# The last feed-forward layer moves into the attention track, as products with tokens on partitions

## What is computed

```python
# layer 3, attention: ctx is 77 x 128, one head over all 128 features
x1 = relu(layernorm(x) @ W.T) * diagonal;  x2 = relu(ctx @ W.T)
x  = x + tanh(g_xattn[3]) * softmax(x1 @ x2.T + mask) @ ctx
# layer 3, feed-forward: 8 experts of 128 x 128, the two largest router weights are kept
y  = layernorm(x);  r = softmax(y @ W_router.T + b_router);  w = r where r is among its two largest, else 0
x  = x + tanh(g_ffn[3]) * sum_e w[:, e] * (y @ W_experts[e].T + b_experts[e])
```

## Time and profile before

| | us |
|---|---|
| median of 3 runs (lowest, highest) | 1231.35 (1228.35, 1235.36) |
| the profiled execution: its time | 1217.92 |
| the profiled execution: its span | 1216.2 |
| PE busy | 1002.3 (82%) |
| DVE busy | 688.4 (57%) |
| ACT busy | 461.2 (38%) |
| chain that ended last: PE, DVE, ACT | 56%, 24%, 9% |

### The profile page before, as it was taken

One profiled execution on the slowest core, in us unless ns is written; L12 is line 12 of the kernel. 1 busy time (PEld: TensorE's weight loads), 2 busy tenths in 40 slices (PEclk: granted clock), 3 DMA queues, 4 the chain that ended last, 5 costly groups with the idle time before them and its releaser, 6 DMA issues.

```text
span 1216.2 us, 14249 instructions
## 1 busy us (share of the span) xinstructions
PE 1002.3 (82%) x4727; PEld 642.2 (53%) x4727; DVE 688.4 (57%) x2092; ACT 461.2 (38%) x1097; POOL 105.6 (9%) x174
## 2 busy tenths in 40 slices
PE   2458889887877786875889989989989999999998
PEld 1334444443333465555556656757757677775442
DVE  0761442518266386378364565775775676766542
ACT  0514345357647454445522424425314322221110
POOL 2100000003022021022000000100100010000000
PEclk8569899999687798888898989999999999998765
DMA  9200000000000000000000000000000000000000
GB/s 273 81 1 1 1 1 1 1 1 1 0 1 0 1 1 1 1 1 1 1 1 1 1 1 1 1 1 1 1 1 1 1 1 1 1 1 1 9 9 18
DMA packets 12081, 12.73 MB, mean 10 GB/s; under 512 B 3766, under 2 KB 7912, under 8 KB 12008
## 3 DMA queue, kind: packets, MB, share of 16 engines
q10 hardware_dynamic: 5536, 8.04, 2.3%
q1 hardware_dynamic: 6088, 3.24, 1.0%
q0 software_dynamic: 384, 0.53, 0.2%
HBM read 10.75 MB, written 1.05 MB: 10 GB/s over the span
## 4 chain that ended last, share of the span: by engine, by line
PE 56%; DVE 24%; ACT 9%; issue 3%; POOL 1%; ACTq 0%; DVEq 0%
PE bank L1540 8%; PE bank L1528 5%; PE bank L1447 5%; PE bank L1530 4%; PE bank L1529 4%; DVE hb L1240 4%; PE bank L1582 4%; DVE nm L1105 3%; PE bank L1333 3%; PE bank L1467 3%; DVE hb L1244 3%; DVE x L1229 2%; ACT PTs L904 2%; ACT hb L938 2%; PE bank L1345 2%
## 5 line engine op out<-in xcount | busy, mean ns | idle before, releaser
L1240 DVE SCALAR_TENSOR_TENSOR hb<-hb,bank 96x512 f32<-96x512 f32 (+1 forms) x160 | 109.3, 683 | 177.1 <-ACT hb L938 176.6
L938 ACT ACTIVATE hb<-bank 96x512 f32<-96x512 f32 (+1 forms) x160 | 95.2, 595 | 291.2 <-PE bank L1530 291.0
L1540 PEld LDWEIGHTS bank<-m_w,hb 128*128 128x128 f32 (+1 forms) x1280 | 173.5, 199 | 24.5 <-DVE x L1229 6.0
L1540 PE MATMUL bank<-m_w,hb 128*128 128x128 f32 (+1 forms) x1280 | 176.6, 283 | 1.0
L1528 PE MATMUL bank<-parts,m_w_lo 128*96 128x512 f32 (+1 forms) x320 | 150.3, 470 | 13.0 <-DVE hb L1240 13.0
L1529 PE MATMUL bank<-parts,m_w_hi 128*96 128x512 f32 (+1 forms) x320 | 133.2, 416 | 0.0
L1530 PE MATMUL bank<-parts,m_w_hi 128*96 128x512 f32 (+1 forms) x320 | 132.9, 415 | 0.0
L1345 PE MATMUL bank<-KT,Qs 96*128 96x308 f32 x192 | 78.1, 425 | 42.5 <-ACT PTs L851 21.2
L1244 DVE TENSOR_TENSOR hb<-hb,bank 96x512 f32<-96x512 f32 (+1 forms) x160 | 109.7, 686 | 5.5
L1467 PE MATMUL bank<-Qs,KT 112*77 112x512 f32 x192 | 95.3, 527 | 16.5 <-ACT PTs L904 14.3
L1105 DVE TENSOR_REDUCE nm<-bank 128x4 f32<-128x308 f32 x192 | 83.6, 470 | 14.7 <-PE bank L1349 7.8
(11 more groups left out here) (269 smaller groups left out, 1530.2 us busy)
## 6 DMA issues: line engine op xcount, KB each, us to landing
nat_m<-in_L_ffn_W_dram ACTq DMA_DIRECT2D x1, 1408.0 KB, 16.8
m_w<-in_L_ffn_w_dram ACTq DMA_DIRECT2D x1, 1024.0 KB, 10.8
raw_w<-in_L_ffn_w_dram ACTq DMA_DIRECT2D x1, 1024.0 KB, 11.9
x<-in_x_dram SPq DMA_DIRECT2D x4, 256.0 KB, 9.0
out_dram<-x SPq DMA_DIRECT2D x4, 256.0 KB, 2.0
f_out<-in_L_ffn_Wout_dram POOLq DMA_DIRECT2D x8, 64.0 KB, 7.5
m_w<-in_L_ffn_W_experts_dram ACTq DMA_DIRECT2D x1, 512.0 KB, 16.6
ctxn<-in_ctx_dram SPq DMA_DIRECT2D x4, 38.5 KB
```

The lines of the kernel that those rows point to most:

```text
L938: act.activation(hb[n % 3][0:m, :], bank[TURN[0]][0:m, :], ACT.Tanh, scale=0.5).then_inc(*chunk_act.up(u, n))
L1240: dve.scalar_tensor_tensor(out=h, in0=h, scalar=1.0, in1=bank[TURN[0]][0:m, :], op0=ALU.add, op1=ALU.mult) \
L1540: op = pe.matmul(bank[7][:, t * P:(t + 1) * P], hb[n % 3][0:m, t * P:(t + 1) * P], wd, start=i == 0 and t == 0, stop=ends_expert(k, n) and ...
```

## The change

Layer 3 leaves the feed-forward track. The attention track now has the twelve attention halves of layers 0 to 2 and then, for each stream in turn, its layer-3 attention half and its layer-3 feed-forward half: A12 is layer-3 attention of stream 0, A13 layer-3 feed-forward of stream 0, A14 and A15 are those of stream 1, A16 and A17 of stream 2, A18 and A19 of stream 3. Beside F10 now lie four halves of that track (A12 to A15), beside F11 two (A16, A17), and A18 and A19 follow alone.

A layer-3 feed-forward half now has tokens on partitions. For each of the four tiles of 128 tokens and each group of four experts (`E3`), PE makes one 128 x 512 product in three fp32r passes into bank 0 or 1. DVE adds its four 128-column parts to `x`, each with its own token weight, in four instructions that wait for one another. The bias is one addition ahead of them. The gate is now folded into the token weights.

The weights `m3_w` get a high and a low part. To make room, `raw_w3` now lies in the memory of `m1_w2`, and the load of `m1_w2` is issued by ACT later, when POOL has read `raw_w3` for the last time.

```diff
+ATTENTIONS = 3 * STREAMS
 def kind(u):
     half, i = u
+    if half == "A" and i >= ATTENTIONS:
+        return "F3" if (i - ATTENTIONS) % 2 else "A3"
     return half + str(i // STREAMS)
...
-            raw_w3 = tmp("raw_w3", [P, MOE1, F1])[:]
+            raw_w3 = m1_w2[:].rearrange("p e c d -> p e (c d)")
...
-            grouped("m3", [(nat_e[:, e, :], m3_w[:, e, :]) for e in range(MOE3)])
+            split += split_parts("m3", nat_e, m3_w, MOE3)
...
                 act.dma_start(nat_m3[:], a["L2_ffn_W3"].rearrange("e m n -> m e n")).then_inc(*landed["m2_w3"].up("all", by=16))
-                act.dma_start(m1_w2[:], a["L1_ffn_w2"].rearrange("e (c p) d -> p e c d", p=P)) \
-                    .then_inc(*landed["rest"].up("all", by=16))
                 act.dma_start(graw[:, 0, :], a["g_xattn"].partition_broadcast(P)).then_inc(*landed["gates"].up(by=16))
...
                     if i == m2_last:
+                        act.wait_ge(*m1_low.at("m1_w3"))
+                        act.dma_start(m1_w2[:], a["L1_ffn_w2"].rearrange("e (c p) d -> p e c d", p=P)) \
+                            .then_inc(*landed["rest"].up("all", by=16))
...
-    parts = two("parts", [P, 3, N], F32R)
-    gT = [q[0:2 * EMAX, 2, :] for q in parts]
+    parts = two("parts", [P, 2, N], F32R)
+    xf_hi = [q[:, 0, :] for q in parts] + [Qs[:, 1, :]]
+    xf_lo = [q[:, 1, :] for q in parts] + [Qs[:, 2, :]]
+    gT = xfa[0:MOE3, :]
...
+    E3 = 4
+    tiles = [(t, e) for t in range(T) for e in range(0, MOE3, E3)]
...
+    beside = [[i + LAG] for i in range(ATTENTIONS - LAG)] + [[12, 13, 14, 15], [16, 17]]
...
-        for i in range(HALVES):
-            if i + LAG < HALVES:
-                yield from merged(weights_a(("A", i + LAG)), [1.0] * steps_f(("F", i)))
-            else:
-                yield from "F" * steps_f(("F", i))
+        for i in range(ATTENTIONS):
+            yield from merged([w for j in beside[i] for w in weights_a(("A", j))], [1.0] * steps_f(("F", i)))
+        for j in (18, 19):
+            yield from "A" * len(weights_a(("A", j)))
...
                 if k == "F3":
-                    for e in range(MOE3):
-                        dve.wait_ge(*share_psum.at(u, e))
...
-                        dve.tensor_tensor(xw[e % 2], xff[s][:], bank[TURN[e % 2]][:], ALU.mult).then_inc(*share_used.up(u, e))
+                    dve.wait_ge(*ffn_psum.at(u, "bias"))
+                    dve.tensor_tensor(x[b][:].rearrange("p t d -> p (t d)"), bank[3][:],
+                                      x[b][:].rearrange("p t d -> p (t d)"), ALU.add).then_inc(*x_done.up(u, "bias"))
+                    dve.wait_ge(*x_done.at(u, "bias"))
+                    for n, (t, e) in enumerate(tiles):
+                        dve.wait_ge(*chunk_psum.at(u, n))
+                        for j in range(E3):
+                            if e + j:
+                                dve.wait_ge(*x_done.at(u, t, e + j - 1))
+                            dve.scalar_tensor_tensor(out=x[b][:, t, :], in0=bank[n % 2][:, j * P:(j + 1) * P],
+                                                     scalar=gw[s][:, t, e + j:e + j + 1], in1=x[b][:, t, :],
+                                                     op0=ALU.mult, op1=ALU.add).then_inc(*x_done.up(u, t, e + j))
                         yield
...
+                    for t in range(T):
+                        op = pe.matmul(bank[3][:, t * P:(t + 1) * P], gT[:, t * P:(t + 1) * P], m3_b[:], start=t == 0, stop=t == T - 1)
...
+                    for n, (t, e) in enumerate(tiles):
+                        d = n % 2
                         free(d)
-                        pe.matmul(bank[d][:], pick[k][:, e:e + 1].to_broadcast([2 * MOE3, P]), gT[s], start=True, stop=True) \
-                            .then_inc(*share_psum.up(u, e))
...
-                            pe.matmul(bank[7][:], m3_w[:, e - 1, :], xw[(e - 1) % 2], start=False, stop=False) \
-                                .then_inc(*ffn_psum.up(u, e - 1))
+                        for xp, wp in ((xf_lo, 0), (xf_hi, 1), (xf_hi, 0)):
+                            op = pe.matmul(bank[d][:], xp[s][:, t * P:(t + 1) * P], m3_w[wp][:, e * P:(e + E3) * P],
+                                           start=xp is xf_lo, stop=xp is xf_hi and wp == 0)
+                        op.then_inc(*chunk_psum.up(u, n))
+                        reader[d] = (x_done, u, t, e + E3 - 1)
                         yield
```

More of the change, by code:

```diff
@@ L90, in source @@
         return ("A", i)
+    if i >= ATTENTIONS:
+        return ("A", i - 1) if kind(u) == "F3" else ("F", ATTENTIONS - STREAMS + stream(u))
     return ("F", i - STREAMS) if i >= STREAMS else None
@@ L568, in two, with three @@
         return [sb(f"{name}{s}", shape, dt) for s in range(SIDES)]
+    def three(name, shape, dt=F32):
+        return [sb(f"{name}{s}", shape, dt) for s in range(SIDES + 1)]
     def each(name, shape, dt=F32):
@@ L594, in main @@
     top = sb("top", [P, T, 8])
-    chosen = sb("chosen", [P, T, LG])
-    gw = two("gw", [P, T, EMAX])
-    gp = two("gp", [P, T, 2 * EMAX])
-    gs = two("gs", [P, 2, T])
+    chosen = {half: sb(f"chosen_{half}", [P, T, LG]) for half in "AF"}
+    gw = three("gw", [P, T, EMAX])
+    gs = three("gs", [P, 2, T])
     gs3 = sb("gs3", [P, 2, T])
@@ L692, in steps_body @@
             return H + 1
-        return {"A3": 3, "F0": C0 + 1, "F3": MOE3 + 1}.get(k) or len(chunks[k]) + LATE
+        return {"A3": 3, "F0": C0 + 1, "F3": len(tiles)}.get(k) or len(chunks[k]) + LATE
     def steps_tail(k):
-        return 7 if k in MHA else 2 if k in ("F0", "F3") else 0
+        return 7 if k in MHA else 2 if k == "F0" else 0
     def weights_a(u):
@@ L723, in attention @@
         def attention():
-            for i in range(HALVES):
+            for i in range(ATTENTIONS + 2 * STREAMS):
                 u = ("A", i)
@@ L882, in pre @@
                         E = router[k][2]
[L883 removed]
+                        if i == 5:
                             act.wait_ge(*xf_ready.at(u))
@@ L942, in body @@
                 if k == "F3":
-                    for _ in range(MOE3 + 1):
+                    for _ in tiles:
                         yield
```

117 lines of the change are left out of this document (45 added, 72 removed).

## The result

The changed kernel takes 1236.33 us (median of 20 runs, 1227.02 to 1243.49), the kernel before 1230.07 on the same chip (20 runs, 1219.25 to 1237.2). The ratio is 1.0055, 95% interval 1.0032 to 1.0078: slower by 6 to 7 us where 12 us less were forecast. The profiled execution took 1235.71 us.

What follows compares the result with a forecast made beforehand. PE was taken to set the pace in layer 2 and, at a lower clock, in F12 to F15. The end (-3.5) and the beginning (-8.5) made -12 us: 1231.35 - 12 = 1219.4 us, range 1198 to 1238.

Steps and rivals of the forecast that it cites:

- The beginning: Start of the program up to ACT's first copy: m1_w2 no longer loads ahead of the gates, net -8.5 us.
- rival (a): Start of the program: the queue gives nothing, the gates wait for nat_m3 anyway; -2.8 us, 1228.5; chance 0.17.
- The additions: DVE's 32 dependent additions in a layer-3 feed-forward half: 0.375 us each, 12.0 us a half.
- the 50 us: From F10 to the end: what the stage should gain by PE's work alone, 50 us.
- The end of the program: F10 to the span's end: 964.2 + 122 + 80 + 46.5 = 1212.7 against 1216.2, so -3.5 us.
- F10 122: F10 with A12 to A15 beside it: 122 us, bounds 95 and 140.
- So DVE becomes the bound: F10 with A12 to A15: DVE's work 95 us against PE's 86.5, so DVE sets the pace.
- F11 80: F11 with A16 and A17 beside it: 80 us, bounds 74.5 and 90.
- The tail 46.5: A18 and A19 alone with the store: 18, 26 and 2.5 us, together 46.5, bounds 42 and 52.
- (b): F10 and F11: PE's gaps lower its clock; at 0.68 the net is +23 us, 1254; chance 0.13.
- (c): Good overlap: F10 takes 95, F11 74.5, the tail 46.5; -44.5 us, 1187; chance 0.12.
- (d): Layer-3 feed-forward halves: additions are quick, 8.3 us a half, in all -15 us, 1204.6; chance 0.05.

Runs made afterwards that it cites:

- e1: The kernel before with only the load of m1_w2 moved to later, layer 3 unchanged: 1213.18 us, ratio 0.9898.
- e12: The same kernel as e1 (the kernel before with only the moved load), run a second time: 1217.88 us, ratio 0.9925.
- e4: The changed kernel with one addition of four in each tile, the other experts' shares left out of the result: 1219.84 us, ratio 0.9941.
- e5: The changed kernel with one fp32r product of three in each tile, the two with low parts left out: 1236.18 us, ratio 1.008.
- e9: The changed kernel with extra bf16 matmuls behind PE's steps in A18 and A19, on a bank nothing reads: 1231.55 us, ratio 1.0068.
- e3: The changed kernel with tiles of two token columns by two experts, so each addition waits for the one before the last: 1227.42 us, ratio 0.9984.
- e7: The changed kernel with layer 3's new feed-forward form put back in the feed-forward track, with tiles of two by two: 1211.99 us, ratio 0.9879.

## Why the prediction was wrong

**Right.** The beginning: forecast -8.5, and A0 starts 9.1 us earlier. The size is partly luck, for the 9.2 in it was only the middle between 4.3 and 14. The issue of the gates did not wait for `nat_m3` (it ended at 24.06, the load landed at 34.2), so rival (a) is out. Room in the queue fits, but what the remaining 4.58 us wait for is not shown. The gain stays to the end (e1, e12). The additions: forecast 0.375 apart and 12.0 a half, measured 0.385 and 12.4 (32 from 1219.14 to 1231.55). The medians as base were right as well: the profiled execution of before was a quick one.

**Read wrongly, with little effect.** DVE's free time in F10 was not "at most 1 us at a time": its longest wait for ACT was 2.6 us. The period of 2.37 is that of undisturbed chunks; over F10 the mean distance was 66.1 / 23 = 2.87. And the 50 us that PE's work alone was to give come from no sum; the text's own terms make 65.27 + 66.50 + 101.42 before and 86.5 + 74.5 + 13.2 after, 59 less.

**Wrong: "The end of the program: 964.2 + 122 + 80 + 46.5 = 1212.7 against 1216.2, so -3.5 us".** It was +15.5. Its three terms were each too small:

- *F10 122: measured 126.6 (+4.6).* "So DVE becomes the bound" is the step that failed in its mechanism. The forecast wanted DVE above 75% and PE below; it was 71% and 81%. PE's work was the term sized too small: it was busy for 102.4 us where the sum had 86.5, while DVE had 89.5 for 95. About half of the difference is in the chunk products, which by their four lines take 93.3 us at the granted clock of 0.91 and took 85.2 at 1.00. To PE's 102.4 come 24.2 in which it waits, mostly at preparation steps that stand behind another half's work, and at the end of F10 tiles that fall where no chunk is prepared. e4 and e5 show that neither DVE's additions nor PE's products set most of the gaps. The number came out near by luck: 122 was added up from handovers by chunk and left 35.5 us beyond the 86.5 of PE's work. The work was 16 more and the waits were 11 less, and the two errors nearly cancel.
- *F11 80: measured 87.2 (+7.2).* "+8" counted only the tiles of A17, by the chunks that they stand in. The eleven preparation steps that A17 adds were put at nothing beyond PE's work. F11's 23 gaps grew by 13.5 us, and with fewer additions (e4) 10.7 of these remain. That the preparation steps make these 10.7 is argued from F10, not shown.
- *The tail 46.5: measured 53.7 (+7.2).* A18 took 21.0 for 18, A19 29.0 for 26, and 1.3 lie between F11's last expert sum and A18's statistics. I had worked A18's steps out from A14's, which ran beside F12's work, and did not ask what the clock would be where PE is alone and mostly idle. At 0.91 A18 takes 18.2 us (e9), my figure. So 3 of the 7 are the clock, which I had as a rival for F10 and F11 only. In A19 the largest miss is "gates and bias 3.4": from the last token weight (1213.49) to the first addition (1219.14) it took 5.65.

Together 19.0, and -3.5 + 19.0 = 15.5.

**The rivals.** (b), the clock in F10 and F11, did not come in its size: 0.91 and 0.96, far from 0.75. (c), good overlap: no; nothing here came near PE's 86.5. (d): quick additions would be worth 11.8 us of the end in the four halves (e3), of the 15 that I had for it. The Trainium skill ("VectorE: DVE Perf Modes", the errata for TRN2) has a cycle count of 120 plus the columns for a PSUM source at 0.96 GHz, from which I estimate (120 + 128) / 0.96 = 258 ns; the alternating additions are near it (17.6 us for 64 in the row below, 0.275 each), the dependent ones are not.

DVE's groups by line from 1100 us on, first of the changed kernel, then of e3_two_rows:

```profile
L1262 DVE SCALAR_TENSOR_TENSOR x<-bank,gw,x 128x128 f32<-128x128 f32 x64 | 22.0, 350 | 3.4 <-PE bank L1590 1.1
```

```profile
L1263 DVE SCALAR_TENSOR_TENSOR x<-bank,gw,x 128x128 f32<-128x128 f32 x64 | 17.6, 344 | 1.9 <-PE bank L1592 1.7
```

One addition lasts about the same, 0.34 to 0.35. Only the start of the next moves forward when it needn't wait for this one.

The fastest version is e7: the new form, its additions alternating, in the feed-forward track, with the moved load. It is 1.2% faster than the kernel before, in two runs. Of this, 0.75 to 1.0 points are the moved load alone (e12, e1). The intervals of the two overlap, so the form's own part rests on the ends alone (251.3 and 249.4 against 242.7 and 238.9).

## What to carry to other kernels

When work is merged into another half's track, don't price it by the engine with the most work alone: here both had time free, at 81% and 71%, and the stretch took 126.6 us all the same. List its steps that go from one engine to another and back, look at what stands ahead of each in the other queue, and ask what the host half has left to do at its end. A change of two independent parts should be timed part by part: here the small one was the gain. And a stretch where one stream stands alone is to be priced at the lower clock, with durations from rows at that clock.
